# A decoder layer in which the second group's sigmoids move to exp and VectorE, and the last batch's softmax and the tile tables are re-ordered

## The reference, cut to what matters

```python
# linear attention: 16 heads of width 8
h = x @ Wh + bh
q = sigmoid(x @ Wq + bq); k = sigmoid(x @ Wk + bk); v = x @ Wv + bv
kv  = einsum('bndh,bnmh->bdmh', k, v)
num = einsum('bndh,bdmh->bnmh', q, kv); den = einsum('bndh,bdh->bnh', q, k.sum(1))
out = relu((layernorm(num / den) * ln_w + ln_b) * (h + beta) @ Wo + bo)
# cross attention: 16 heads of width 64, keys and values from the context
probs = softmax(q @ k.T / 8); out = (probs @ v) @ Wo + bo
# feed-forward: a shared expert, and one of 8 routed experts per token (top 1)
out = swiglu(x, shared) + swiglu(x * sigmoid(top logit), expert[argmax])
```

## Time and profile before

| what | value |
|---|---|
| runs of the kernel before | 607.21 us median, 606.89 to 608.82 (n = 3) |
| the profiled execution, its own time | 606.39 us |
| its span in the profile | 604.7 us |
| mean granted TensorE clock | 0.994 |
| PE busy | 576.7 us (95%) |
| DVE busy | 432.2 us (71%) |
| ACT busy | 432.0 us (71%) |
| POOL busy | 311.9 us (52%) |

### The profile page before, as it was taken

How to read it: one execution, slowest core, us unless ns; L and a number is a source line. 1 busy time by engine, 2 the same in 40 slices (tenths; PEclk the granted TensorE clock), 3 DMA queues, 4 the chain that set the end, 5 groups by cost and what they waited for, 6 DMA issues and landing times.

```text
span 604.7 us, 15181 instructions
## 1 busy us (share of the span) xinstructions
PE 576.7 (95%) x5479; PEld 528.7 (87%) x5479; DVE 432.2 (71%) x1210; ACT 432.0 (71%) x1514; POOL 311.9 (52%) x332
## 2 busy tenths in 40 slices
PE   8978999999999999999999999999999999899993
PEld 8867998988999899989998889989998988788993
DVE  4869666877685858776876787767856558589773
ACT  2668778786877777677867687768777876665881
POOL 3545553365336643675347525655464326445774
PEclk9999999999999999999999999999999999999997
DMA  6530000100010000010000000000220201242530
GB/s 158 141 65 14 18 3 1 31 2 2 1 33 17 21 2 14 19 38 1 14 20 27 11 5 11 19 19 3 89 70 20 66 8 36 82 129 76 150 103 19
DMA packets 24955, 23.52 MB, mean 39 GB/s; under 512 B 7007, under 2 KB 22497, under 8 KB 24880
## 3 DMA queue, kind: packets, MB, share of 16 engines
q1 hardware_dynamic: 21520, 15.96, 10.2%
q0 software_dynamic: 2784, 6.32, 3.0%
q10 hardware_dynamic: 576, 0.26, 0.2%
HBM read 15.03 MB, written 7.95 MB: 38 GB/s over the span
## 4 chain that ended last, share of the span: by engine, by line
PE 66%; ACT 16%; DVE 10%; issue 2%; POOL 2%; DMA 2%; SPq 1%; POOLq 0%; DVEq 0%; ACTq 0%
PE bank L1408 8%; PE bank L1376 8%; PE bank L1397 8%; PE bank L1386 7%; PE bank L1237 7%; ACT prob L1111 7%; PE bank L1239 6%; PE bank L1238 6%; PE bank L1522 4%; PE bank L1539 2%; PE bank L1255 2%; PE bank L1357 2%; ACT probT L1117 2%; DMA prob<-in_L_xattn_Wk_dram 2%; PE bank L1243 1%
## 5 line engine op out<-in xcount | busy, mean ns | idle before, releaser
L1111 ACT ACTIVATE prob<-bank,mneg 128x128 f32<-128x128 f32 x512 | 183.4, 388 | 63.3 <-DVE mneg L860 63.1
L599 POOL TENSOR_TENSOR prob<-prob,rden 128x512 f32<-128x512 f32 x128 | 131.1, 1045 | 104.2 <-DVE rden L867 104.0
L1111 ACT ACTIVATION_READ_ACCUMULATOR prob<-bank,mneg 128x1 f32 x512 | 115.8, 226 | 0.0
L1117 ACT COPY probT<-bank 128x512 f32<-128x512 f32 x128 | 77.9, 609 | 19.3 <-PE bank L1386 18.7
L860 DVE TENSOR_REDUCE mneg<-bank 128x4 f32<-128x512 f32 x128 | 83.1, 670 | 2.5 <-PE bank L1376 2.5
L1386 PE MATMUL bank<-ident,prob 128*128 128x128 f32 x512 | 78.6, 276 | 3.4 <-POOL prob L599 2.0
L538 POOL TENSOR_TENSOR rstd<-var_eps,neg_half 128x4 f32<-128x4 f32 x24 | 24.7, 1030 | 97.5 <-DVE var_eps L694 97.5
L1386 PEld LDWEIGHTS bank<-ident,prob 128*128 128x128 f32 x512 | 59.6, 142 | 10.5 <-ACT probT L1117 3.1
L1376 PE MATMUL bank<-kT,qT 64*128 64x128 f32 x1024 | 66.2, 279 | 0.4 <-ACT prob L1111 0.4
L1376 PEld LDWEIGHTS bank<-kT,qT 64*128 64x128 f32 x1024 | 59.8, 188 | 6.3 <-issue 2.5
L1408 PE MATMUL bank<-xwo,oT 128*128 128x128 f32 x512 | 63.7, 277 | 0.5 <-ACT oT L1121 0.5
(11 more groups left out here) (224 smaller groups left out, 1389.7 us busy)
## 6 DMA issues: line engine op xcount, KB each, us to landing
prob<-routed SPq DMA_DIRECT2D x39, 128.5 KB, 2.2
s_work<-in_x_dram SPq DMA_DIRECT2D x8, 256.0 KB, 2.9
ctx_nat<-in_ctx_dram SPq DMA_DIRECT2D x8, 192.0 KB, 2.7
routed<-blank SPq DMA_DIRECT2D x9, 128.5 KB, 4.1
s_work<-in_L_ffn_rt_gate_dram SPq DMA_DIRECT2D x1, 1024.0 KB, 5.5
s_work<-in_L_ffn_rt_up_dram SPq DMA_DIRECT2D x1, 1024.0 KB, 9.5
prob<-in_L_xattn_Wq_dram SPq DMA_DIRECT2D x1, 512.0 KB, 6.9
xwo<-in_L_xattn_Wo_dram SPq DMA_DIRECT2D x1, 512.0 KB, 9.2
```

The lines of the kernel that those rows point to most:

```text
L599: nc.gpsimd.tensor_tensor(view, view, spread(rden[:, m % 2, c * NC:(c + 1) * NC], 2, S), ALU.mult)\
L1111: last = nc.scalar.activation(prob[:, m % 2, p * S:(p + 1) * S], score_bank[c][:, i * S:(i + 1) * S], ACT.Exp, bias=mneg[:, m % 2, p:p + 1 ...
L1117: nc.scalar.copy(probT[:, m % 2, c * 512:(c + 1) * 512], made(r1, ("T", m, c))[:])\
```

## The change

**The second group's sigmoids.** For g = 1 ACT computes exp(-k) and exp(-(q + bq)), with a negated bias that it makes once, and DVE finishes the sigmoid as 1 / (1 + e) in a new step "second sigmoids": two additions of 1 and two reciprocals, each over 128 x 512 values, each addition linked to its reciprocal by a wait. This step stands at beat (-1, 3) on DVE, and the exponentials at (-1, 2) on ACT. The group's later steps move back: "k^T v" and "mask" to (0, 0), "q k^T v" and "attention" to (0, 1), both halves of the gating to (0, 2), "turn gated" to (0, 3), "output" and "x1" to (1, 0), "normalise x1" to (1, 1), and "turn x1", "x1^T high" and "x1^T low" to (1, 3). "x^T low" goes from (-2, 3) to (-1, 0), behind the first two row maxima. The exp table is loaded early, behind the first group's "x1^T high". The high and low parts of the shared expert's weights are made at (-2, 2) and (1, 2) and no longer at (-1, 2) and (-1, 3). The other groups keep their sigmoids.

**The last batch.** For batch 31 DVE and not POOL multiplies by the inverse sums (`norm_probs_last`); DVE takes the row maxima of chunks 2 and 3 one beat earlier, ahead of emptying v; ACT takes the exponentials of chunks 1 to 3 ahead of emptying the transposed probabilities of batch 30. Scatters of groups 5 and 6 and group 6's record change their beats.

**The tail.** The last group's feed-forward steps come one tile later (all but "normalise" and "rstd"), and the second table is made in six parts two tiles apart and not in three parts and a rest. The parts' instructions are the same.

```diff
+                (L6 + 1, 3): ("gate and up 1", "tanh 1", "activate 1"),
+                (L6 + 2, 0): ("down", "shared", "record"),
+                (L6 + 2, 1): ("scatter 0", "scatter 1", "scatter 2", "scatter 3")}
+        MOVED.update({(NG - 3, "scatter 2"): (B - 3, 3), (NG - 3, "scatter 3"): (B - 3, 3)})
...
-                 (1, "turn x"): (-2, 3), (1, "copy x^T"): (-2, 3), (1, "x^T low"): (-2, 3),
+                 (1, "turn x"): (-2, 3), (1, "copy x^T"): (-2, 3), (1, "x^T low"): (-1, 0),
                  (1, "project first pair"): (-1, 0), (1, "first pair"): (-1, 0),
-                 (1, "project second pair"): (-1, 1), (1, "second pair"): (-1, 1)})
+                 (1, "project second pair"): (-1, 1), (1, "second pair"): (-1, 1),
+
+                 (1, "sigmoids"): (-1, 2), (1, "k^T v"): (0, 0), (1, "mask"): (0, 0), (1, "q k^T v"): (0, 1),
+                 (1, "attention"): (0, 1), (1, "gate terms"): (0, 0), (1, "rstd of attention"): (0, 1),
+                 (1, "gating, first half"): (0, 2), (1, "gating, second half"): (0, 2),
+                 (1, "turn gated"): (0, 3), (1, "copy gated^T"): (0, 3), (1, "output"): (1, 0), (1, "x1"): (1, 0),
+                 (1, "rstd of x1"): (1, 0), (1, "normalise x1"): (1, 1), (1, "turn x1"): (1, 3),
+                 (1, "x1^T high"): (1, 3), (1, "x1^T low"): (1, 3)})
...
-        PE_TAIL = {3: ["turn h"], 4: ["logits"], 5: ["gate and up 0"], 6: ["rank"], 7: ["gate and up 1"],
-                   9: ["down"]}
...
-        TABLE_STEPS = (7, 8, 10)
+        PE_TAIL = {4: ["turn h"], 5: ["logits"], 6: ["gate and up 0"], 7: ["rank"], 8: ["gate and up 1"],
+                   10: ["down"]}
...
+        POOL_TAIL = {1: ["rstd"], 7: ["record"], 10: ["scatter 0"], 11: ["scatter 1"], 12: ["scatter 2"],
+                     13: ["scatter 3"]}
+
+        TABLE_STEPS = (9, 11, 13, 15, 17, 19)
...
-                    if b == 0 and live(n):
+                    if b == 0 and live(n) and n < B - 1:
                         norm_probs(n, 2)
                         norm_probs(n, 3)
-                    if b == 2 and live(n + 1):
+                    if b == 2 and live(n + 1) and n + 1 < B - 1:
                         norm_probs(n + 1, 0)
...
+                if step == "second sigmoids":
+                    dve.wait_ge(exp_1, 1)
+                    v = hkv[:, :, D:2 * D]
+                    link(nc.vector.tensor_scalar(v, v, 1.0, None, ALU.add))
+                    nc.vector.reciprocal(v, v).then_inc(sig_1, 1)
+                    dve.wait_ge(*r1.freed((g, 5)))
+                    link(nc.vector.tensor_scalar(qsT[:], qsT[:], 1.0, None, ALU.add))
+                    nc.vector.reciprocal(qsT[:], qsT[:]).then_inc(sig_1, 1)
...
+            def norm_probs_last(c):
+                dve.wait_ge(rec_done, 2 * (B - 1) + c // 2 + 1)
+                cols, p = slice(c * NC * S, (c + 1) * NC * S), (B - 1) % 2
+                view = prob[:, p, cols].rearrange("p (h k) -> p h k", k=S)
+                nc.vector.tensor_tensor(view, view, spread(rden[:, p, c * NC:(c + 1) * NC], 2, S), ALU.mult)\
+                    .then_inc(norm_last, 1)
...
                     if (n, b) == (B - 1, 0):
+                        norm_probs_last(2)
+                        norm_probs_last(3)
                         fill_first_table()
+                    if (n, b) == (B - 2, 1):
+
+                        row_max(n + 1, 2)
+                        row_max(n + 1, 3)
                     if b == 2 and live(n + 1):
                         reciprocal(n + 1, 0)
-                    if b == 2 and live(n + 1):
+                    if (n, b) == (B - 2, 2):
+                        norm_probs_last(0)
+                        norm_probs_last(1)
...
+                    if (n, b) == (-1, 3):
+                        s1(1, "second sigmoids")
...
-                if j == TABLE_STEPS[-1] + 3:
-                    rows_written()
...
-                if step == "sigmoids":
+                if step == "sigmoids" and g == 1:
+                    act.wait_ge(*r1.freed((g, 4)))
+                    nc.scalar.activation(hkv[:, :, D:2 * D], hkv[:, :, D:2 * D], ACT.Exp, scale=-1.0).then_inc(exp_1, 1)
+                    ps = made(r1, (g, 5))
+                    act.wait_ge(bq_turned, 1)
+                    nc.scalar.activation(qsT[:], ps[:], ACT.Exp, scale=-1.0, bias=bq_neg[:])\
+                        .then_inc(r1.emptied["s1_act"], 1)
+                if step == "sigmoids" and g != 1:
...
+                    if g == 0:
+
+                        nc.scalar.activation(table_first[:], neg_half[:], ACT.Exp)
...
-                    if (n, b) == (-1, 2):
+                    if (n, b) == (-2, 2):
                         act.wait_ge(wm_in, 16 * 4)
                         nc.scalar.copy(sh_gu_hi[:], rawgu).then_inc(wm_hi, 1)
-                    if live(n):
+
+                    exps_first = n == B - 2 and b > 0
+                    if live(n) and not exps_first:
                         empty_T(n, b)
...
                     if live(n + 1) and b == NC - 1:
                         exp_chunk(n + 1, b)
+                    if exps_first:
+                        empty_T(n, b)
...
-                    pe.wait_ge(k_sig, g + 1)
+                    if g == 1:
+                        pe.wait_ge(sig_1, 1)
+                    else:
+                        pe.wait_ge(k_sig, max(g, 1))
...
-                    pe.wait_ge(*r1.freed((g, 5)))
+                    pe.wait_ge(*((sig_1, 2) if g == 1 else r1.freed((g, 5))))
```

More of the change, by code:

```diff
@@ L104, in decoder_layer @@
         bq_col = sb("bq_col", [P, 1])
+        bq_neg = sb("bq_neg", [P, 1])
         b_hkv = sb("b_hkv", [P, 3 * D])
@@ L351, in steps_at @@
                     if MOVED.get((g, step), (a + slot, int(beat))) == (n, b)]
-        PE_TAIL = {3: ["turn h"], 4: ["logits"], 5: ["gate and up 0"], 6: ["rank"], 7: ["gate and up 1"],
-                   9: ["down"]}
[L356 to L360, removed]
-        TABLE_STEPS = (7, 8, 10)
+        PE_TAIL = {4: ["turn h"], 5: ["logits"], 6: ["gate and up 0"], 7: ["rank"], 8: ["gate and up 1"],
+                   10: ["down"]}
+        ACT_TAIL = {4: ["copy h^T"], 6: ["score", "tanh 0"], 8: ["tanh 1"]}
+        DVE_TAIL = {2: ["normalise"], 4: ["h^T low"], 5: ["route"], 6: ["activate 0"], 7: ["rows"], 8: ["activate 1"],
+                    10: ["shared"]}
+        POOL_TAIL = {1: ["rstd"], 7: ["record"], 10: ["scatter 0"], 11: ["scatter 1"], 12: ["scatter 2"],
+                     13: ["scatter 3"]}
+        TABLE_STEPS = (9, 11, 13, 15, 17, 19)
         S1_BANKS = {"turn x": [(0, "s1_dve")], "project first pair": [(1, "s1_dve"), (2, "s1_dve")],
@@ L912, in count_tiles, with pass_experts, fill_weights @@
                                                op0=ALU.mult, op1=ALU.add)
+            def pass_experts(tiles):
                 entry(nc.vector.tensor_tensor(passed[:, 0:tiles, :], spread(tiles_to[:], 1, tiles),
                                               tile_no[:, 0:tiles, :], ALU.is_le))
-            def fill_table(half, tiles):
+            def fill_weights(half, tiles):
                 entry(nc.vector.tensor_reduce(t_expert[:, 0:tiles], passed[:, 0:tiles, :], AX.X, ALU.add))
@@ L922, in fill_table, with fill_rows @@
                                         ALU.min, ALU.mult)
+            def fill_rows(half, tiles):
                 entry(nc.vector.tensor_tensor(skipped[:, 0:tiles, :], passed[:, 0:tiles, :],
@@ new lines, in second_table @@
+                if part_ == 1:
+                    add_tiles(ROUND2)
+                if part_ == 2:
+                    pass_experts(ROUND2)
+                    fill_weights(1, ROUND2)
+                if part_ == 3:
+                    fill_rows(1, ROUND2)
+                    assert entries[0] == TABLE_2
+                if part_ == 4:
+                    entry(nc.vector.tensor_tensor(stride[:], begun[:, 1:], begun[:, 0:E], ALU.subtract))
+                    entry(nc.vector.tensor_tensor(skipped[:, 0:ROUND2, :], passed[:, 0:ROUND2, :],
+                                                  spread(stride[:], 1, ROUND2), ALU.mult))
+                    entry(nc.vector.tensor_reduce(t_expert[:, 0:ROUND2], skipped[:, 0:ROUND2, :], AX.X, ALU.add))
@@ new lines, in second_table @@
+                if part_ == 5:
+                    entry(nc.vector.scalar_tensor_tensor(out=t_row[:, 0:ROUND2], in0=t_expert[:, 0:ROUND2],
+                                                         scalar=begun[:, 0:1], in1=t_row[:, 0:ROUND2], op0=ALU.add,
+                                                         op1=ALU.subtract))
+                    entry(nc.vector.tensor_scalar(written[:], t_row[:, 0:ROUND2], lane[:], float(TOKENS), ALU.is_gt,
+                                                  ALU.mult))
@@ L995, in _ @@
                         row_max(n + 1, 1)
-                    if b == 1 and live(n + 1):
+                    if b == 1 and live(n + 1) and n < B - 2:
                         row_max(n + 1, 2)
```

45 lines of the change are left out of this document (22 added, 23 removed).

## The result

The changed kernel takes 615.14 us (median of 4 runs, 612.85 to 616.29) against 607.47 (4 runs): a ratio of 1.0122, 95% interval 1.0090 to 1.0153. That is +7.7 us where +2.9 was forecast, and outside the range on record (603.5 to 613.0). The direction was right, the size was not. The profiled execution took 615.85 us, span 614.1, against 606.39 and 604.7: by the two spans the difference is 9.4 us, as before's profiled execution lies under its median and after's above.

What follows compares the result with a forecast made beforehand. The prediction took PE, busy 95% of the span, as the bound, so added waits are never caught up. Its terms, +5.9 + 1.9 - 2.4 - 1.0 - 1.5 = +2.9 us, gave 610.1 against 607.21, range 603.5 to 613.0.

Steps and rivals of the forecast that it cites:

- The start's sum: Start: 5.9 us lag up to batch 1's first transpose plus 1.9 us for the late x1.
- x1^T's wait: Slot 2: the q product waits for ACT's cast, now behind batch 2's last chunk; costs 1.9 us, bounds 0 and 2.4.
- VectorE's chain: Start: second sigmoids (8.1 us) then 12.1 us of VectorE work end the gating at 64.7 us; lag 5.9 us.
- the break-even: Start against end: start loss equals end gain at a reciprocal of 2.1 us, 4 ns a value.
- fast reciprocal: Rival, chance 0.16: about 1 ns a value; start gains 2.5, x1 costs 1.9, end gives 4.9: -5.5 us, 601.7.
- v behind x1: Slot (1, 1): x1 stands ahead of v's emptying; costed at nothing (0 to 0.6 us), as PE has three other products.
- The last batch, 2.4: Batch 31: PE's waits on POOL and ACT go, the first table comes sooner; gain 2.4 us (1.4 to 2.8).
- "Turn h": Tail: its 0.96 us wait for DVE's normalise is covered by other products one tile later; gain 1.0 us.
- the tables, 1.5: Tail: second table in six parts, 1.8 us lost before, 0.3 left; gain 1.5 us (0.8 to 1.8).
- They will leave near 558.6 ... just in time: Second round's loads leave 3.0 us behind scatter 3, near 558.6, with tile 21 two microseconds off.
- just fits: Tail: POOL, issuing a transfer every 1.28 us, starts its last at 591.4 where PE's side asks for 592.7.
- a tail that gives half: Rival, chance 0.1: POOL or the second round's loads hold the tail; only 2.4 us come back: +5.4, 612.6.

Runs made afterwards that it cites:

- The fills: The changed kernel with identity products (10, 10 and 6) put into three of TensorE's waits; 611.67 us against 607.39 before, ratio 1.0068.
- ScalarE's sigmoids: The changed kernel with the second group's sigmoids on ScalarE's own table as before, all steps at the later beats; 613.28 us, 1.0098 of before.
- the end's part alone: The kernel before with only the last batch's softmax, turn of h and tables changed, start as before; 604.17 us against 607.18, ratio 0.9953.
- POOL's order mended: The end's changes on the kernel before, with last-group scatters two to a tile from tile 10, each pair behind that tile's write; 602.26 us, 0.9923.
- the two with the wait filled: The end's changes, scatters paired ahead of writes, plus 8 identity products in TensorE's wait for the second group's sigmoids; 603.25 us (0.9936), on a slow chip 618.17 (0.9958).
- the run with additions: The changed kernel with its two reciprocals over 128x512 values replaced by additions of 1; 624.56 us against 620.80 before, ratio 1.0060.
- the run with the scatters first: The end's changes on the kernel before, last-group scatters two to a tile ahead of that tile's write; 603.27 us (0.9936), on a slow chip 618.68 (0.9973).

## Why the prediction was wrong

- **The step that failed: each wait counted at its length only, the clock at nothing.** The start's sum was 5.9 + 1.9 = 7.8 us, from "From 60 us to 500 us ... a PE wait added ahead of it is never caught up", and it has no term for TensorE's clock: the term was put at nothing without a reason. The start cost 12.5 us. After the new waits the products behind them run at 1.2 GHz, and where those are on the path, as at 65 to 70 and 84 to 90 us, that is time again. The fills took 3.6 us off the lag (12.5 to 8.9), 1.6 of it between the scores of batches 3 and 4 (14.9 against 13.3 us), and the filled kernel's 611.67 us lies inside the range on record. With the waits filled the lag at batch 4 is 8.6 (95.95 against 87.38), for a forecast of 7.8.
- **The instants of the start were right, in part by luck.** The gating ended at 65.1 (64.7), TensorE was at batch 1's first transpose at 66.1, or 65.0 with the waits filled (65.2), and x1^T's wait was 1.8 (1.9). But the new sigmoids took VectorE 7.5 us and not 8.1, and what follows them up to the end of the gating 13.1 and not 12.1 (52.0 to 65.1): two errors that in part cancel. And with ScalarE's sigmoids, without those 7.5 us, "turn gated" is at 64.13 all the same.
- **What to blame in the start was half wrong.** The forecast put 5.9 us to VectorE's chain, with the break-even at a reciprocal of 2.1 us: every microsecond of the two reciprocals was to come back. With additions of 1.15 and 0.43 us in place of 3.35 each, its rule gives about -5.5 us, the rival "fast reciprocal"; measured are a lag of 8.0 us and +3.8 us in time. The rival counted on 2.0 us of a freed wait, and TensorE waits there 2.0 us for POOL instead; and it took the later beats to cost 1.9 us (x1) where alone they lag 10.1.
- **v behind x1 at nothing** (0 to 0.6): it waits 0.6 us, the upper bound.
- **The last batch, 2.4:** 1.8 in the whole change, 2.0 to 2.4 alone. The multiplications are 0.65 us each (0.69 forecast). The table's 2.66 us instruction takes 0.24 now, as forecast; but another of the table's, 1.22 us, ran beside POOL instead.
- **"Turn h", 1.0, and the tables, 1.5:** measured 1.4 and 1.8. In the end's part alone the tiles keep to 1.45 us from tile 11 to 18, so the parts are all hidden. With the last batch's 1.8 for 2.4 the three terms are each off by 0.3 to 0.6 us, and their sum, 5.0 for 4.9, is right because the errors cancel.
- **"They will leave near 558.6 ... just in time":** the second round's loads. This is the second failed step. The end alone has them leave at 561.32 (lag 1.1), and 1.7 to 1.9 us of the gain go. Scatter 0 was put at 547.9 by adding one tile's time; it left at 550.36 in that run, since POOL's write of an earlier tile and the late "shared" stand ahead. Without that wait and with POOL's order mended the end gives 4.9 us.
- **POOL "just fits":** it does in the change as made (the last write is set by PE's tiles, late as they are), and stops fitting once the loads are in time.
- **In sum:** +2.9, and 3.6 for the clock, and a remainder of 1.1 in the start, of which v is 0.6 and the rest is not traced, and 1.9 for the loads less 0.1 for the other terms of the end, make +9.4, which is what the two profiles differ by. The medians' 7.7 is 1.7 less, in part because before's one profile has no fall of the clock at its start. Ten more traces are of kernels with that same start. The eight without a fill all have a fall, at 45 to 50 or at 55 to 60 us, and lags from 0.1 to 2.0 us; the two with the wait filled have none, and lags of 0.65.

The range had no case for it. Its upper end was built from the start's forecast and a tail that gives half; nothing in it let the start itself cost more than its waits.

## What to carry to other kernels

A wait that is new on a saturated TensorE costs its own length and can cost a stretch at half clock behind it; here the two were 7.6 and 4.9 us. Price both, and look at what stands behind the wait: work that ends in another wait hides the slow clock, work that ends in nothing does not. Moving steps to later beats to hide a slow operation is no gift where the beats they move into are themselves short of slack: test the move without the operation. And where one queue issues both the writes and what the next loads wait for, the order in that queue is worth as much as the tables that were made in smaller parts: 1.8 us here (0.9953 against 0.9923), for two changed places.

## What was not expected of the hardware

- **The granted clock** fell to half after waits of 2 to 6 us in this kernel, but not after every one, and at different places in different executions of the same code (0.83 in 40 to 50 us in one run of the end's part, 0.71 in 55 to 60 in another, neither in the profile of before, which has a wait of 2.03 us too).
- **A reciprocal** took 3352 ns for 512 values, 354 for 32 and 196 for 8: (3352 - 354) / 480 = 6.2 ns a value over the whole range. An addition in place over the same 512 values took 0.36 to 0.43 us, and once 1.15, in the run with additions, while POOL was multiplying.
- **Two chips** run the kernel before in 620 us, not 607. The traces from them are like the others up to the scores of the last batch. From there to its output product the last batch's change gains 0.5 to 0.9 us on them and 1.7 to 2.0 on the others, and the tail is longer. The chain of waits of the run with the scatters first, there:

```profile
554.63 3.46 another core or an unknown queue
558.11 0.38 ACT oT L1262
...
560.34 3.46 another core or an unknown queue
563.82 0.14 ACT oT L1262
```

ScalarE stands 3.46 us twice just behind a copy of weights, for something that no row names; the granted clock behind is 0.58 and 0.73 (560 to 565, 565 to 570 us), and from 576 us on every third or fourth tile waits 0.7 to 1.2 us for ScalarE's copy. Every trace from these two chips has such stops in the tail, of up to 2.3 to 4.2 us; none from the others has. The cause stays open; no run was made to look for it.
